# Two of four input tiles turned by a load instead of by TensorE, in a layer of linear attention beside a mixture-of-depths block

## What is computed

```python
def _layernorm(x, axis=-1, eps=1e-05):
    m = jnp.mean(x, axis=axis, keepdims=True)
    v = jnp.var(x, axis=axis, keepdims=True)
    return (x - m) / jnp.sqrt(v + eps)

xn = _layernorm(x)
x = x + attention(xn, ...) + ffn(xn, ...)

# attention: 16 heads of 32, linear attention with a decay per head
qkvu = xn @ W_qkvu.T                  # 512 -> 4 * 512, split into q, k, v, u
q, k = silu(q), silu(k)
# per block of tokens, with a state kv per head
out   = (q * q_decay) @ kv + ((q @ k.T) * diag_decay) @ v
kv    = block_decay * kv + (k * k_decay).T @ v
o     = rms_norm(out) * u
return o @ W_out.T

# ffn: a router xn @ w_router picks the 256 best tokens; they go through softmax
# attention (16 heads of 128, 8 for keys and values, rotary) and a gated MLP, and
# take the place of xn in their rows
```

## Time and profile before

| | us |
|---|---|
| median of 3 runs | 474.69 |
| lowest, highest | 474.67, 475.38 |
| profiled execution, its own time | 474.24 |
| its span in the profile | 472.4 |
| mean granted TensorE clock | 0.999 of full speed |

### The profile page before, as it was taken

The page is one execution under the profiler, slowest core; times in us unless marked ns, Lnnn a source line. Parts: engine busy times, 40 slices in busy tenths (PEclk is TensorE's granted clock), DMA queues, the critical chain, the costliest instruction groups (busy, mean ns, idle before and its releaser), DMA issues. The chain is left out here.

```text
span 472.4 us, 11902 instructions
## 1 busy us (share of the span) xinstructions
PE 462.2 (98%) x4839; PEld 420.9 (89%) x4839; DVE 298.2 (63%) x638; ACT 229.2 (49%) x400; POOL 191.5 (41%) x193
## 2 busy tenths in 40 slices
PE   7999999999999999999999999999999999999994
PEld 7999899998998989989989889988888878999993
DVE  5689776887499999865358778776653335230231
ACT  5951333322276678232442465565566547544430
POOL 3240251101120232041269758542361334689862
PEclk9999999999999999999999999999999999999999
DMA  7967575233521212121830769865758712655403
GB/s 232 399 152 126 122 169 114 78 105 112 170 79 62 66 36 79 48 64 61 302 135 2 268 241 336 318 220 179 240 171 280 263 52 89 170 188 193 142 1 44
DMA packets 40951, 72.14 MB, mean 153 GB/s; under 512 B 5872, under 2 KB 7424, under 8 KB 40768
## 3 DMA queue, kind: packets, MB, share of 16 engines
q1 hardware_dynamic: 40352, 70.06, 46.9%
q0 software_dynamic: 544, 1.31, 1.5%
HBM read 54.03 MB, written 17.32 MB: 151 GB/s over the span
## 5 line engine op out<-in xcount | busy, mean ns | idle before, releaser
L1181 POOL TENSOR_TENSOR wlo<-raw,whi 128x512 fp32r<-128x512 f32 x96 | 124.0, 1325 | 84.7 <-ACT whi L564 84.7
L1255 PE MATMUL banks<-HTh,whi 128*128 128x256 f32 x224 | 65.1, 291 | 0.0
L1257 PE MATMUL banks<-HTh,wlo 128*128 128x256 f32 x224 | 63.3, 283 | 0.0
L1256 PE MATMUL banks<-HTl,whi 128*128 128x256 f32 x224 | 63.3, 283 | 0.0
L845 DVE TENSOR_TENSOR A<-banks,DEC 128x512 f32<-128x512 f32 x64 | 39.7, 682 | 29.2 <-PE banks L1328 27.8
L1160 POOL TENSOR_TENSOR state_dec<-state,small 128x128 f32<-128x128 f32 x16 | 8.4, 526 | 114.1 <-DVE state L856 114.1
L564 ACT ACTIVATE whi<-raw 128x2048 fp32r<-128x2048 f32 x24 | 45.8, 1908 | 10.2 <-PE banks L1257 7.2
L1255 PEld LDWEIGHTS banks<-HTh,whi 128*128 128x128 f32 x224 | 42.9, 191 | 1.2 <-issue 0.6
L1256 PEld LDWEIGHTS banks<-HTl,whi 128*128 128x128 f32 x224 | 42.9, 191 | 0.3
L1257 PEld LDWEIGHTS banks<-HTh,wlo 128*128 128x128 f32 x224 | 42.9, 191 | 0.0
L1308 PE MATMUL banks<-xTh,WUh 128*128 128x256 f32 x128 | 37.5, 293 | 0.0
(11 more groups left out here) (242 smaller groups left out, 1297.6 us busy)
## 6 DMA issues: line engine op xcount, KB each, us to landing
X<-in_x SPq DMA_DIRECT2D x16, 256.0 KB, 6.0
xn_all<-XN SPq DMA_DIRECT2D x16, 256.0 KB, 6.3
uo_all<-park_h SPq DMA_DIRECT2D x16, 256.0 KB, 2.1
uo_all<-park_l SPq DMA_DIRECT2D x16, 256.0 KB, 3.4
raw<-in_wq SPq DMA_DIRECT2D x4, 1024.0 KB, 7.2
uoh<-uo_all SPq DMA_DIRECT2D x16, 256.0 KB, 3.2
uol<-uo_all SPq DMA_DIRECT2D x16, 256.0 KB, 4.2
XR<-in_x SPq DMA_DIRECT2D x16, 256.0 KB, 3.9
```

The source lines that it names most:

```text
L1181: ins = Q.tensor_tensor(low[:, k, :], raw[b % 3][:, k, :], high[:, k, :].bitcast(f32), ALU.subtract)
L1255: T.matmul(dst, lh, rh, start=first, stop=False)
L1256: T.matmul(dst, lh, rl, start=False, stop=False)
L1257: return T.matmul(dst, ll, rh, start=False, stop=last)
```

## The change

Tiles 2 and 3 go the second way: they are loaded turned, and normalised by `turned_norm` with the stored means and deviations. On TensorE the two groups of transpositions in slots -2 and -1 are gone. On SP, the stores of means and deviations and `load_turned` of tiles 2 and 3 stand behind the load of X 4 and ahead of the stores of `XN` 0 to 3. On VectorE `turned_norm` of both tiles comes behind the low part of the U weights, and both `xt_low` behind the statistics of tile 4. On ScalarE `xt_high` of tiles 2 and 3 stand before and after the evacuation of the first U tile. `load_turned(4)` and `(5)` now also wait for `xt_lo`.

```diff
--- before.py
+++ after.py
@@ -354,10 +354,10 @@
 
             def load_turned(M):
 
-                if M >= NXN + 2:
+                if M >= CH + 2:
                     sp.wait_ge(xt_lo, M - 1)
                 sp.dma_start(XA[:, M % 2].rearrange("p k t -> p (k t)"), xT_t[M]).then_inc(xa_in[M % 2], 16)
-                sp.wait_ge(ln_out[M % NXN], 16 * (M // NXN))
+                sp.wait_ge(ln_out[M % NXN], 16 * (M // NXN + (M % NXN >= CH)))
                 sp.dma_start(MR[:, M % 2, :], ln_all[M].partition_broadcast(P)).then_inc(xa_in[M % 2], 16)
 
             def store_uo(N):
@@ -418,6 +418,10 @@
             sp.dma_start(wr_b[:], w_router.partition_broadcast(P)).then_inc(wr_in, 16)
             sp.dma_start(raw_w["U"][:], WT_v[:, :, 3 * DM:4 * DM]).then_inc(w_raw["U"], 16)
             load_x(4)
+            for M in range(CH, NXN):
+                store_ln(M)
+            for M in range(CH, NXN):
+                load_turned(M)
             for M in range(NXN):
                 store_xn(M)
             load_x(NXN + 1)
@@ -503,11 +507,11 @@
                 S.activation(Woh[:], raw_out[:], ACT.Copy).then_inc(o_w_hi, 1)
 
             def xt_high(M):
-                if M < NXN:
+                if M < CH:
                     act.wait_ge(xt_ps, M + 1)
                     src = tiles4(xt_bank(M)[:])
                 else:
-                    act.wait_ge(xt_ok, M - NXN + 1)
+                    act.wait_ge(xt_ok, M - CH + 1)
                     src = XA[:, M % 2]
                 act.wait_ge(proj_ps, NPROJ * max(M // CH - 1, 0))
                 S.activation(xTh[:, M // CH % 2, :, M % CH * P:(M % CH + 1) * P], src, ACT.Copy).then_inc(xt_hi, 1)
@@ -625,12 +629,16 @@
                     block_hi(1)
                 if N == N_TILES - 2:
                     block_hi(3)
-                if N + XT_AHEAD < N_TILES:
+                if NXN <= N + XT_AHEAD < N_TILES:
                     xt_high(N + XT_AHEAD)
                 count_marks(ranked(N, 1))
                 if N == -2:
                     weights_hi("U", u_w_hi)
+                if N == -1:
+                    xt_high(CH)
                 in_position(N, 2, tiles)
+                if N == -1:
+                    xt_high(NXN - 1)
                 if N == N_TILES - 2:
                     mean_square(N - 1)
                 if N == N_TILES - 1:
@@ -743,7 +751,7 @@
                 dve.wait_ge(rstd_ok, M + 1)
                 if M >= NXN:
                     dve.wait_ge(xn_out[M % NXN], 16 * (M // NXN)), dve.wait_ge(score_ok, M - NXN + 1)
-                    dve.wait_ge(xt_ps, min(M - NXN + 1, NXN))
+                    dve.wait_ge(xt_ps, min(M - NXN + 1, CH))
                 V.tensor_scalar(XN[M % NXN][:], X[s][:], mv[:, M, 0:1], rstd[:, M:M + 1], ALU.subtract,
                                 ALU.mult).then_inc(xn_ok, 1)
 
@@ -764,17 +772,17 @@
             def xt_low(M):
                 at = slice(M % CH * P, (M % CH + 1) * P)
                 dve.wait_ge(xt_hi, M + 1)
-                src = tiles4(xt_bank(M)[:]) if M < NXN else XA[:, M % 2]
+                src = tiles4(xt_bank(M)[:]) if M < CH else XA[:, M % 2]
                 V.tensor_tensor(xTl[:, M // CH % 2, :, at], src, xTh[:, M // CH % 2, :, at].bitcast(f32),
                                 ALU.subtract).then_inc(xt_lo, 1)
 
             def turned_norm(M):
 
-                dve.wait_ge(xa_in[M % 2], 32 * ((M - NXN) // 2 + 1))
+                dve.wait_ge(xa_in[M % 2], 32 * ((M - CH) // 2 + 1))
                 both = MR[:, M % 2, :].rearrange("p (m t) -> p m t", t=2)
                 V.tensor_tensor(XA[:, M % 2], XA[:, M % 2], both[:, :, 0].unsqueeze(1).to_broadcast([P, NK, P]),
                                 ALU.subtract).then_inc(xt_sub, 1)
-                dve.wait_ge(xt_sub, M - NXN + 1)
+                dve.wait_ge(xt_sub, M - CH + 1)
                 V.tensor_tensor(XA[:, M % 2], XA[:, M % 2], both[:, :, 1].unsqueeze(1).to_broadcast([P, NK, P]),
                                 ALU.mult).then_inc(xt_ok, 1)
 
@@ -967,16 +975,17 @@
             for M in range(CH, NXN):
                 ln_norm(M)
             first_weights_lo("V", v_w_hi, v_w_lo)
+            first_weights_lo("U", u_w_hi, u_w_lo)
+            for M in range(CH, NXN):
+                turned_norm(M)
+            ln_stats(NXN)
             xt_low(CH)
-            first_weights_lo("U", u_w_hi, u_w_lo)
-            ln_stats(NXN)
+            xt_low(NXN - 1)
             router(0)
             ln_norm(NXN)
             for N in slots_of_chunks:
                 if N >= 0:
                     mask(N)
-                if N == -1:
-                    xt_low(N + XT_AHEAD)
                 if N == INDEX:
                     token_indices()
                 if 1 <= N < N_TILES - CH:
@@ -1486,11 +1495,7 @@
                 if N < 0:
                     in_position(N, 0)
                     in_position(N, 1)
-                    if N == -1:
-                        transposed(N + XT_AHEAD)
                     in_position(N, 2)
-                    if N == -2:
-                        transposed(N + XT_AHEAD)
                     in_position(N, 3)
                     continue
                 score(N)
```

## The result

| | us |
|---|---|
| before, median of 5 (lowest, highest) | 475.05 (474.67, 475.38) |
| changed, median of 5 (lowest, highest) | 477.92 (477.18, 478.37) |
| changed over before | 1.006, 95% interval 1.0047 to 1.0072 |
| profiled execution of the changed kernel: own time, span | 478.37, 476.6 |

The change costs 2.87 us (477.92 - 475.05), or 0.6%; 2.5 were forecast. The profiled execution is the slowest of the five.

A forecast was written before the change was run, and what follows sets the result against it. TensorE, busy 462.2 of 472.4 us, was taken as the bound, with 0.74 us slack before chunk 1's scores. Terms -0.88 + 1.0 + 2.4 = +2.5 on 474.69 gave 477.2 us, range 475.4 to 479.3.

The forecast's parts named there:

- The slack of 0.74 ahead of the scores of chunk 1: Before the change, ScalarE's squares end at 48.08 and TensorE starts the scores of chunk 1 at 48.82: 0.74 us to spare.
- the sum as lateness less slack: The total loss of +2.5 us, also obtained as VectorE's lateness 3.23 less the slack 0.74.
- VectorE late by 3.23: VectorE 3.23 us late from 30.7 on: 2.18 with every load in time, plus 1.05 waiting for the last MR.
- The 1.05 for the last `MR`: VectorE, ready at 28.15, waits 1.05 us for tile 3's MR, landing at 29.2 by the median load time.
- ScalarE's half between the two U tiles included: Before the projection of tiles 2 and 3: VectorE has xTl at 32.9, TensorE asks at 34.0; no wait.
- Transpositions, -0.88: On TensorE, removing two groups of four transpositions saves 0.44 us each, 0.88 in all, unless something else is late.
- The tie holds; I count nothing: At the U projection, TensorE arrives at 26.93 and the low half of the U weights is done about 26.83; no cost.
- First wait 1.0: TensorE asks for the decayed keys at 44.43, VectorE ends them at 45.43: a wait of 1.0 us.
- second 2.4: TensorE reaches the scores of chunk 1 at 48.94, the squares end at 51.31: a wait of 2.4 us.
- The masks and the projection of tiles 2 and 3 made no wait: Masks end at 42.8, before the attention at 43.1; xTl is ready at 32.9, before the projection at 34.0.
- From chunk 1 on nothing more is lost: Behind the scores of chunk 1 VectorE waits for them as before, both engines are in step, and no further time is lost.
- X 5 to X 8 at nothing: Loads X 5 to X 8, later on SP's queue, were costed at nothing, with 0.5 us allowed if either is late.

The follow-up runs named there:

- e14: The changed kernel run once more, unchanged, for a second profile; 477.26 us beside 474.84 for the kernel before (ratio 1.0052).
- e3: The changed kernel with turned_norm of tiles 2 and 3 over 8 of 128 columns only; 478.38 us beside 474.75 (ratio 1.0074).
- e4: The changed kernel with xt_high of tile 3 ahead of the evacuation of the first U tile on ScalarE; 478.57 us beside 474.75 (1.0071).
- e5: The changed kernel with both turned_norm over 8 columns and xt_high of tile 3 ahead of the first U evacuation; 479.23 us beside 474.75 (1.0092).
- e10: The kernel before with four extra chained VectorE operations (0.71 us each) behind the low part of the U weights; 477.50 us beside 475.19 (1.0045).
- e7: The kernel before with only SP's queue order changed, adding stores and loads for tiles 2 and 3 that nothing reads; 477.33 us beside 475.19 (1.0046).
- e1: The changed kernel with VectorE's decayed keys and gated outputs moved earlier in slot 0; 477.99 us beside 475.19 (1.0054).
- e12: The kernel of e1 with the turned load of tile 5 ahead of slot 0's transfers on SP's queue; 476.27 us beside 474.84 (1.0033).
- e13: The kernel of e12 with xt_high of tile 3 ahead of the first U evacuation and the raw_out load behind X 9; 476.61 us beside 474.84 (1.0044).
- e8: The kernel before with only one of the four transpositions of tiles 2 and 3 each; 474.62 us beside 474.84 (1.0001).
- e2: The kernel before with decayed keys and gated outputs moved earlier on VectorE in slot 0, as a control; 474.81 us beside 475.19 (0.9986).
- e6: The changed kernel with 11 idle matmuls of 0.21 us on TensorE ahead of the scores of chunk 1; 478.51 us beside 474.75 (1.0083).

## Why the prediction was right, and where it was not

The forecast had the mechanism right: VectorE is late, and TensorE waits for the squares of chunk 0. The size came out partly by luck, as the points below say. The mechanism shows when the end of the squares is set beside the start of the scores of chunk 1, in us:

| run | squares done | scores of chunk 1 | from chunk 0 to 1 |
|---|---|---|---|
| before | 48.08 | 48.82 | 15.18 |
| changed | 51.05 | 51.19 | 17.85 |
| e14 (changed again) | 51.65 | 51.80 | 17.86 |
| e3 | 51.47 | 51.61 | 17.87 |
| e4 | 51.68 | 51.85 | 17.68 |
| e5 | 50.68 | 50.83 | 17.14 |
| e10 | 51.13 | 51.27 | 17.34 |
| e7 | 50.81 | 51.06 | 16.45 |
| e1 | 48.02 | 48.60 | 15.34 |
| e12 | 48.40 | 50.30 | 16.93 |
| e13 | 48.38 | 49.96 | 16.14 |

In the changed kernel, e14, e3, e5 and e10 the scores start 0.14 or 0.15 behind the squares, whatever pauses TensorE had before; in e4 and e7 TensorE arrives at about the same time by itself. In e1, e12 and e13 the squares come early, and they don't hold it. The start of chunk 0 differs between the profiles, from 33.26 (e1) to 34.61 (e7); the last column leaves this out, and by it both profiles of the changed kernel lose 2.7.

- **The slack of 0.74 ahead of the scores of chunk 1, and the sum as lateness less slack: right.** 2.96 - 0.74 = 2.2, and the trace has 2.37; the rest is the 0.14 that TensorE takes to go on behind the squares, which the slack left out. e10 gives lateness alone and gets 2.45, e1 takes the dependence away and chunk 1 starts on time.
- **VectorE late by 3.23: 2.96, right in size and wrong in its parts.** The 1.05 for the last `MR` wasn't there: it was issued at 22.87, as worked out within 0.4, and landed after 5.2 us, at 28.1, between the least and the median of the earlier trace rows. The Trainium skill's formula ("DMA: Bandwidth & Descriptors", Anatomy of one DMA), which is for DMAs issued by GpSimd, gives an estimate of 2.3 and is off by more than half, though its consequence, no wait, came true. That the lateness still came out near is luck: in the place of the 1.05 came 0.2 of a wait for `xTh` of tile 3, 0.2 in front of the normalisation of tile 4, and 0.4 since the low half of the U weights was done at 27.26 instead of 26.83. The order on ScalarE was half a sentence in the forecast, "ScalarE's half between the two U tiles included"; by e3 it is a bound of its own, equal to the work.
- **Transpositions, -0.88: the failed term.** "The tie holds; I count nothing" was the step. The low half of the U weights comes from ScalarE's high half, and TensorE can't pass it: in the first profile 0.30 is left at chunk 0, in e14 the scores of chunk 0 start 0.30 later than before (33.94), and in e8 nothing can be measured. I counted the lead of TensorE and not that of the weights. The total hardly feels it, since what TensorE wins ahead of chunk 0 it waits longer for the squares.
- **First wait 1.0, second 2.4:** 0.2 and 2.45. TensorE came to the new keys 0.6 later than in the forecast, by the failed term, and the decayed keys were done 0.3 earlier (45.17). The masks and the projection of tiles 2 and 3 made no wait, as said.
- **"From chunk 1 on nothing more is lost": right in e14 (2.98, 2.96), wrong in the first profile**, where the fall of the clock took 1.55 more.
- **X 5 to X 8 at nothing:** true in the profile, but only just. X 8 was issued at 39.54 (33.95 before), took 3.9 to land, and VectorE read it at 43.46, at once. e5 and e7, in which VectorE is earlier, show that the cover is gone: waits of 0.92 and 1.56. So VectorE's lateness and the moved transfers lie side by side; each costs over 2 us alone (e10, e7), and together they cost little more than one. For e7 that is the measured time; by which way its queue costs it is shown only in part, as said there.

**What stays open** is the pause inside the row of matmuls for the new keys in slot 0. There is none over 0.3 in the profiles of the kernel before, e1, e2, e3, e8 and the first one of the changed kernel; it is in those of e4, e5, e6, e7, e10, e12, e13 and e14. In e12 it is what is left: 5.25 from the new keys to the scores of chunk 1 (50.30 - 45.05) instead of 3.51. In e1, e3 and e5 a pause of 0.85 to 1.05 stands in the same row of slot 3, where the distance grows by 1.1 to 1.4. It comes with the moved loads alone (e7) and with VectorE's lateness alone (e10). More data moves beside it: 60 to 228 GB/s during the longest pause of slot 0 in e4, e5, e6, e7, e10, e12, e13 and e14, and 15 to 54 GB/s during the row in the kernel before, e1, e3 and the first profile of the changed one. That TensorE's instructions arrive late beside these transfers would fit, but it is a guess: no run here moved the instruction supply by itself.

## What to carry to other kernels

Work taken from the busiest engine and put on one with much idle time is paid for by the slack at the next place where the two meet: find that place and its slack first, here 0.74 us, and compare it with the added work. Look for every chain that ends there (the added operations, the order on a third engine, the loads behind a held queue): three of them had nearly the same length here, so undoing one or two gave nothing back in the time. A wait for a small store in the middle of a DMA queue holds all that is issued behind it; here X 8 went out over 5 us later.

## What the runs showed of the hardware that I had not expected

TensorE's granted clock fell to half for 3.4 us, from 1.3 and 1.4 us after it resumed from an idle time of 2.45 (changed) and of 2.3 us (e3), at a cost of 1.5 us each time. From 12 us on, the engine had had no other break of over 0.7 us. Behind an idle time of 1.7 us (e1) the clock stayed at full speed. A 1 KB store took 3.9 us to land when nothing else was in the queue (kernel before, issued at 29.66) and 8.1 us behind a transfer of 1 MB (e7, issued at 30.73).
